# Attention in one launch: value products one half step at a time, maxima turned by VectorE, sums copied in halves

## The reference

```python
qkv = x @ W_attn + b_attn
q, k, v = jnp.split(qkv, 3, axis=2)
...
scores = jnp.einsum('bhqd,bhkd->bhqk', qh, kh) * scale
scores = jnp.where(causal, scores, -jnp.inf)
probs = jax.nn.softmax(scores, axis=-1)
out = jnp.einsum('bhqk,bhkd->bhqd', probs, vh)
out = out.transpose(0, 2, 1, 3).reshape(B, S, D)
return out @ W_proj + b_proj
```

## Time and profile before

| | |
|---|---|
| three runs | 2105.65, 2110.08, 2115.99 us; median 2110.08 |
| profiled execution | 2109.09 us, its span 2107.4 us |
| PE busy | 2033.5 us (96%) |
| DVE busy | 1854.7 us (88%) |
| ACT busy | 1486.4 us (71%) |
| POOL busy | 475.0 us (23%) |
| exponentials, L1021 | 2176, 596 ns mean |
| maxima, L1047 | 960, 1220 ns mean |
| value products, L1232 | 8696 instructions, 694.6 us |
| DMAs on the SP queue | 157.92 MB, 25.9% of the 16 DMA engines' time |

### The profile page before, as it was taken

One profiled execution on the slowest core, in us unless ns is written; L12 is line 12 of the kernel. 1 busy time (PEld: TensorE's weight loads), 2 busy tenths in 40 slices (PEclk: granted clock), 3 DMA queues, 4 the chain that ended last, 5 costly groups with the idle time before them and its releaser, 6 DMA issues. The chain is left out here.

```text
span 2107.4 us, 46575 instructions
## 1 busy us (share of the span) xinstructions
PE 2033.5 (96%) x18225; PEld 1126.7 (53%) x18225; DVE 1854.7 (88%) x3143; ACT 1486.4 (71%) x2787; POOL 475.0 (23%) x637
## 2 busy tenths in 40 slices
PE   6987999999999999999999999999999989999998
PEld 5875444444444444444444444444444458888887
DVE  7988799999999999999999999999999738998996
ACT  2331388888888888888888888888888665555554
POOL 0000011011111111111011111101111127776774
PEclk9997799999999999999999999999999999999999
DMA  6896021121212112122121212212122122323320
GB/s 194 319 324 221 14 71 47 53 58 38 76 46 67 48 48 65 36 77 51 54 58 38 66 47 70 48 53 58 38 76 67 47 74 80 98 86 91 84 77 31
DMA packets 163004, 168.31 MB, mean 80 GB/s; under 512 B 74704, under 2 KB 102880, under 8 KB 162784
## 3 DMA queue, kind: packets, MB, share of 16 engines
q1 hardware_dynamic: 155072, 157.92, 25.9%
q10 hardware_dynamic: 7712, 7.41, 1.2%
HBM read 95.77 MB, written 67.63 MB: 78 GB/s over the span
## 5 line engine op out<-in xcount | busy, mean ns | idle before, releaser
L1021 ACT ACTIVATE probs<-ps_s 128x512 f32<-128x512 f32 x2176 | 1178.7, 596 | 243.2 <-PE ps_s L1211 215.6
L1047 DVE TENSOR_REDUCE maxes<-ps_m 128x2 f32<-128x1024 f32 (+1 forms) x960 | 1142.7, 1220 | 104.9 <-PE ps_m L1174 82.5
L1232 PE MATMUL ps_acc<-probs,vs 128*32 128x256 f32 (+1 forms) x8696 | 694.6, 391 | 11.2 <-ACT acc_sb L999 11.2
L1211 PE MATMUL ps_s<-qs,ks 50*128 50x512 f32 (+3 forms) x2560 | 571.1, 444 | 0.8 <-ACT probs L1021 0.7
L1174 PE MATMUL ps_m<-ks,qs 48*128 48x512 f32 (+3 forms) x2560 | 498.7, 388 | 13.7 <-DVE maxes L1047 8.3
L1211 PEld LDWEIGHTS ps_s<-qs,ks 50*128 50x128 f32 x2560 | 251.4, 183 | 408.4 <-ACT probs L1021 373.4
L1232 PEld LDWEIGHTS ps_acc<-probs,vs 128*32 128x32 f32 x8696 | 172.8, 108 | 290.3 <-issue 188.9
L953 POOL TENSOR_SCALAR_AFFINE_SELECT probs<-probs 128x512 f32<-128x512 f32 x256 | 158.8, 635 | 721.9 <-ACT probs L1021 718.0
L1174 PEld LDWEIGHTS ps_m<-ks,qs 48*128 48x128 f32 x2560 | 260.9, 189 | 90.5 <-DVE maxes L1047 70.9
L1054 DVE CUSTOM_DVE_ANT_0 sums_masked<-ps_m,mask 128x384 f32<-128x384 f32 (+1 forms) x512 | 186.6, 420 | 21.7 <-PE ps_m L1174 5.7
L1425 POOL TENSOR_TENSOR hid<-square,hid 128x512 fp32r<-128x512 f32 x128 | 175.4, 1382 | 97.6 <-DVE square L1436 85.7
(11 more groups left out here) (133 smaller groups left out, 1851.0 us busy)
## 6 DMA issues: line engine op xcount, KB each, us to landing
qs<-q_scr SPq DMA_DIRECT2D x384, 64.0 KB, 2.7
ks<-k_scr SPq DMA_DIRECT2D x384, 64.0 KB, 2.8
q_scr<-probs SPq DMA_DIRECT2D x32, 512.0 KB, 3.9
k_scr<-probs SPq DMA_DIRECT2D x32, 512.0 KB, 5.3
o_scr<-acc_sb SPq DMA_DIRECT2D x64, 256.0 KB, 2.9
v_scr<-probs SPq DMA_DIRECT2D x16, 512.0 KB, 6.0
v_dense<-v_scr SPq DMA_DIRECT2D x16, 512.0 KB, 4.5
o_in<-o_scr SPq DMA_DIRECT2D x32, 256.0 KB
```

The source lines that it names most:

```text
L1021: act.activation(probs[:, s % RING, x], ps_s[:, k % BANKS], ACT.Exp).then_inc(ring_taken, 1)
L1047: last = dve.tensor_reduce(maxes[c % 2][:, :, pairs, tt, i], banks, AX.X, ALU.max)
L1211: last = pe.matmul(ps_s[:, k % BANKS, at:at + width], ks[u][rows, j // TT, p, j % TT * P:(j % TT + 1) * P], qs[u][rows, c, p, q0:q0 + widt ...
L1232: last = pe.matmul(ps_acc[h * VW:(h + 1) * VW, q0:q0 + width], vs[u][:, j, h], probs[:, s % RING, h % banks_of(s), at:at + width], start=( ...
```

## The change

- **Value products.** They are now a list of their own (`VALUES`): two entries for a step of four banks, one for a step of two heads, 68 in all. Each half step does one entry, the one VALUES_BEHIND = 6 half steps back. Halves are 256 and 256 columns, in a mixed step 256 and 128 + 128; a two-head step's 256 are done in one.
- **Rows of maxima.** VectorE turns `max_parts` (128 x 32) in 32 x 32 blocks into `max_rows` (128 x 32: for each 32 queries the 32 rows of maxima). TensorE's transpose and ScalarE's copy go, and the ring holds scores alone. `store_rows` has eight DMAs of 2 KB in place of four of 4 KB: for each of four blocks of 32 queries and each of two row groups, 16 partitions of 128 bytes go into 2 partitions of eight pieces each.
- **Sums of values.** `ps_acc` is copied in two halves of 256 columns: the first after the mixed step's products, the second after the two-head step's, which touch the second half only. The two-head step's products wait for the first copy, the next chunk's first product for the second.

```diff
+VALUES_BEHIND = 6
...
 def halves_of(s):
     blocks = STEPS[s][2]
     j, q0, col, width = blocks[0]
-    if len(blocks) > 1:
-        return [blocks[:1], blocks[1:]]
-    return [[(j, q0, col, width // 2)], [(j, q0 + width // 2, col + width // 2, width // 2)]]
+    return [[(j, q0, col, 2 * P)], [(j, q0 + 2 * P, col + 2 * P, width - 2 * P)] + blocks[1:]]
+VALUES = [(s, halves) for s in range(NS) for halves in ([(0,), (1,)] if banks_of(s) == 4 else [(0, 1)])]
...
+def order(s, last):
+    got = []
+    for half in range(banks_of(s) // 2):
+        x = sum(banks_of(i) // 2 for i in range(s)) + half
+        y = x - VALUES_BEHIND
+        got += [("bank", 2 * half), ("bank", 2 * half + 1), *items_at(x), ("values", (y < 0, *VALUES[y % len(VALUES)]))]
+    return [(what, y) for what, y in got if not (last and what in ("item", "found", "rows") and y[0])]
+def acc_piece(s, halves):
+    if 1 not in halves:
+        return None
+    return 1 if s + 1 in CHUNK_END else 0 if s + 2 in CHUNK_END else None
...
+    sp.wait_ge(lead.acc_copied, 2 * (NCH * n + c + 1))
...
-        max_rows = [t.sb(f"max_rows{i}", [MROWS * GH * TT, P], F32R) for i in range(2)]
+        max_rows = [t.sb(f"max_rows{i}", [P, MROWS * GH * TT], F32R) for i in range(2)]
...
+        rows_turned, rows_in = t.sem("rows_turned"), [t.sem(f"rows_in{i}") for i in range(2)]
...
+        TURN = 32
+        ROWS = 2 * P // TURN
...
-            def store_rows(u, c, copied):
-                sp.wait_ge(ring_taken, copied)
-                for r in range(2):
-                    for a in range(MROWS):
-                        dst = qs[u][ROW * r + TERMS + a:ROW * r + TERMS + a + 1, c].rearrange("o p (t q) -> o (p t) q", q=P)
-                        row = (r * MROWS + a) * PAIRS * TT
-                        sp.dma_start(dst.bitcast(F32), max_rows[c % 2][row:row + PAIRS * TT, :].bitcast(F32)).then_inc(rows_in[c % 2], 16)
+            def store_rows(n, u, c):
+                sp.wait_ge(rows_turned, NCH * n + c + 1)
+                for i in range(P // TURN):
+                    for r in range(2):
+                        dst = qs[u][ROW * r + TERMS:ROW * r + TERMS + MROWS, c].rearrange("a p (t i q) -> a (p t) i q", i=P // TURN, q=TURN)[:, :, i]
+                        row = TURN * i + r * MROWS * PAIRS * TT
+                        sp.dma_start(dst.bitcast(F32), max_rows[c % 2][row:row + MROWS * PAIRS * TT, :].bitcast(F32)).then_inc(rows_in[c % 2], 16)
...
-                    opened += 1
-                    store_rows(0, x[1], opened)
+                    store_rows(0, 0, x[1])
...
-                            store_rows(*unit_of(x, n, u)[1:], taken(n, k))
-                        k += what in ("bank", "rows")
+                            store_rows(*unit_of(x, n, u))
...
-            def copy_rows(n, c, filled, k):
-                act.wait_ge(ring_filled, filled)
-                if not early(n, c):
-                    act.wait_ge(rows_in[c % 2], 16 * 2 * MROWS * halves(n, c))
-                act.copy(max_rows[c % 2][:], ps_s[0:MROWS * GH * TT, k % BANKS, 0:P]).then_inc(ring_taken, 1)
-            def copy_acc(n, c):
-                act.wait_ge(pv_done, NS * n + CHUNK_END[c])
-                if not early(n, c):
-                    act.wait_ge(acc_stored[c % 2], 16 * halves(n, c))
+            def copy_acc(n, s, piece):
+                c = STEPS[s][0]
+                act.wait_ge(pv_done, NS * n + s + 1)
+                if piece == 0 and not early(n, c):
+                    act.wait_ge(lead.acc_stored[c % 2], 16 * halves(n, c))
                     act.wait_ge(lead.sums_in[c % 2], 16 * GH * halves(n, c))
-                act.copy(lead.acc_sb[c % 2][:], ps_acc[:]).then_inc(acc_copied, 1)
-            opened = 0
-            for what, x in OPENING:
-                if what == "rows":
-                    copy_rows(0, x[1], opened + 1, opened)
-                    opened += 1
+                part = slice(2 * P * piece, 2 * P * (piece + 1))
+                act.copy(lead.acc_sb[c % 2][:, part], ps_acc[:, part]).then_inc(acc_copied, 1)
...
-                            unit, _, c = unit_of(x, n, u)
-                            copy_rows(unit, c, taken(n, k), k)
-                            k += 1
-                    if at := ended(s, PV_BEHIND, n, first):
-                        copy_acc(*at)
+                        elif what == "values" and not (first and x[0]):
+                            if (piece := acc_piece(*x[1:])) is not None:
+                                copy_acc(n - 1 if x[0] else n, x[1], piece)
...
+                    for s, parts in VALUES[-VALUES_BEHIND:]:
+                        if (piece := acc_piece(s, parts)) is not None:
+                            copy_acc(n, s, piece)
...
+            def turn_rows(n, c):
+                dve.wait_ge(max_parted, 2 * (NCH * n + c + 1))
+                if not early(n, c):
+                    dve.wait_ge(rows_in[c % 2], 16 * ROWS * halves(n, c))
+                dve.transpose(max_rows[c % 2][:].bitcast(F32),
+                              max_parts[c % 2][:].bitcast(F32).rearrange("p r a x -> p (r a x)")).then_inc(rows_turned, 1)
...
+                            unit, _, c = unit_of(x, n, u)
+                            turn_rows(unit, c)
...
-            def turn_rows(n, c, k):
-                pe.wait_ge(max_parted, 2 * NCH * n + 2 * (c + 1))
-                pe.transpose(ps_s[0:MROWS * GH * TT, k % BANKS, 0:P],
-                             max_parts[c % 2][:].bitcast(F32).rearrange("p r a x -> p (r a x)"), keep["ident"][:]).then_inc(ring_filled, 1)
...
-                    pe.wait_ge(rows_in[c % 2], 16 * 2 * MROWS * (halves(n, c) + 1))
+                    pe.wait_ge(rows_in[c % 2], 16 * ROWS * (halves(n, c) + 1))
...
-                        pe.wait_ge(acc_copied, NCH * n + c)
-                pieces = blocks if halves == (0, 1) else halves_of(s)[halves[0]]
+                        pe.wait_ge(acc_copied, 2 * (NCH * n + c))
+                    if s + 1 in CHUNK_END:
+                        pe.wait_ge(acc_copied, 2 * (NCH * n + c) + 1)
+                pieces = blocks if parts == (0, 1) else halves_of(s)[parts[0]]
                 for j, q0, col, width in pieces:
                     for h in range(GH):
                         at = h // banks_of(s) * (CH // heads) + col
                         last = pe.matmul(ps_acc[h * VW:(h + 1) * VW, q0:q0 + width], vs[u][:, j, h],
                                          probs[:, s % RING, h % banks_of(s), at:at + width],
-                                         start=(j == 0 and 0 in halves), stop=(s + 1 in CHUNK_END), skip_group_check=True)
-                if 1 in halves:
+                                         start=(j == 0 and 0 in parts), stop=(s + 1 in CHUNK_END), skip_group_check=True)
...
-                        elif what == "rows":
-                            unit, _, c = unit_of(x, n, u)
-                            await_bank(n, k, first)
-                            turn_rows(unit, c, k)
-                            k += 1
-                        elif what == "values" and s >= PV_BEHIND:
-                            values(n, u, s - PV_BEHIND, x, last)
+                        elif what == "values" and not x[0]:
+                            values(n, u, *x[1:], last)
                         elif what == "values" and not first:
-                            values(n - 1, 1 - u, NS + s - PV_BEHIND, x, False)
+                            values(n - 1, 1 - u, *x[1:], False)
                         elif what == "values":
                             fill(pe, keep["w_o"], ps_acc[:], 2)
...
-                    for s in range(NS - PV_BEHIND, NS):
-                        values(n, u, s, (0, 1), True)
+                    for s, parts in VALUES[-VALUES_BEHIND:]:
+                        values(n, u, s, parts, True)
```

More of the change, by code:

```diff
@@ L1285, in _ @@
                         fill(pe, keep["w_o"], ps_acc[:], 3)
-                elif what == "rows":
-                    turn_rows(0, x[1], opened)
-                    opened += 1
             def body(n, u, first, last):
```

35 lines of the change are left out of this document (11 added, 24 removed).

## The result

The changed kernel takes 2301.2 us (median of 4 runs, 2283.71 to 2326.53), the kernel before beside it 2110.63 (4 runs, 2105.65 to 2115.99): ratio 1.0875, with an interval of 1.0794 to 1.0956. It is slower, as forecast, but by 190 us instead of 28, and far outside the range of 2085 to 2160. The profiled execution took 2308.57 us, its span is 2306.9.

A forecast was written before the change was run, and what follows sets the result against it. TensorE's order of work was taken as the bound, SyncE's queue directly under it. Per unit, 90.6 - 2.9 + 4.9 of waits = 92.6 us; fifteen units +30, the last -1.35, giving 2138 us, range 2085 to 2160.

The forecast's parts named there:

- c: SyncE's queue: time from one row DMA's issue to the next, taken as 0.65 us, bounds 0.47 and 0.77.
- both waits: TensorE waits 1.55 us for rows before chunk 3's scores, 3.35 for loads before the next unit's chunk 2 maxima: 4.9.
- The 1.8 to a row DMA's landing: SyncE's rows of maxima: the last row DMA lands 1.8 us after its issue starts, as the sums' copy does.
- TensorE's own gain: Attention unit: TensorE's terms sum to -2.9 us, so left to itself it would need 87.7 per unit instead of 90.6.
- the half copies: Accumulator copied in two halves: 0.1 us for each of eight waits, 0.8 per unit, ends 0 and 0.25 each.
- the whole copy: Accumulator copy at chunk ends: its old hold-up of some 1.15 us per unit goes; net -0.35 with the new copies' waits.
- the turn on VectorE: Rows of maxima turned on VectorE: 0.2 us each, bounds nothing and 0.6, costing TensorE nothing but starting row DMAs later.
- the pieces of 128 + 128: Value products of mixed half steps on TensorE: 0.63 us each; re-cutting the pieces takes 6.7 to 6.5, -0.2 per unit.
- the last unit: Last attention unit, which loads no successor: only the first wait, -2.9 + 1.55 = -1.35 us.
- The queue isn't felt: Rival on SyncE: loads get ahead or issue overlaps, only TensorE's gain of 46 us is left, 2064; chance 0.06.
- The issues are cheap: Rival on SyncE: row DMAs cost 0.47 us like loads, waits 2.0, unit 89.7, about 2094; chance 0.12.
- The gain fails as well: Rival: VectorE falls behind or copy waits cost 0.25 each, while the waits stay; 94.5 per unit, 2168; chance 0.13.

The follow-up runs named there:

- e4: The kernel before with each row DMA cut in two (eight of 2 KB per chunk), nothing else: 2287.63 us, ratio 1.0730 to the kernel before.
- e3: The changed kernel with chunk rows turned and sent two half steps earlier and the loads around them moved to either side: 2063.93 us, ratio 0.9769 to the kernel before.
- e6: The kernel before with VectorE's turn, eight row DMAs and e3's places, keeping the old product order and whole copies: 2077.95 us, ratio 0.9859.
- e7: The changed kernel's product order and half copies, with the kernel before's TensorE transposes, ScalarE copies and four row DMAs: 2085.7 us, ratio 0.9889.
- e1: The changed kernel with dummy products of 512 columns, 6 and 13, ahead of its two waits on DMAs: 2167.53 us, ratio 1.0262 to the kernel before.
- e10: e3 with TensorE made to wait once per unit for ScalarE to read the scores just made, no late DMA: 2137.0 us, ratio 1.0090 to the kernel before.
- e11: e3 with TensorE made to wait for ScalarE in three half steps running, once per unit: 2269.16 us, ratio 1.0724 to the kernel before.
- e9: e1 with VectorE's turn of chunk 3's rows put ahead of the ternary weights in the last unit: 2148.77 us, ratio 1.0187 to the kernel before.

## Why the prediction was wrong

**Right, on SyncE.** c = 0.65 held (0.65 to 0.67), and with it the reading of the earlier trace rows that a DMA which leaves SBUF costs the queue more than a load. The queue did set both waits: 1.46 where 1.55 stood, and where 3.35 stood 3.1 to 3.3 in six units (1.2 to 2.8 in three, 4.0 to 5.0 in three, 2.7 on average). The 1.8 to a row DMA's landing was taken from the sums' copy, as no row gives it; it fits here, as the eighth issue begins at about 933.2 and the scores at 935.0. The Trainium skill's sentence in "DMA: Bandwidth & Descriptors", section "Issuing engines are not separate DMA queues", that starting a DMA is "usually small relative to the DMA itself", does not hold here: e4 loses 154 us to four more issues per chunk. In three units (lengths 109.7, 105.4 and 93.5) the second wait was under 0.3, because a low clock behind the first had given the queue time.

**Right, on TensorE's own gain.** 87.7 per unit was predicted; e3 shows 87.8 to 88.4. Of its terms the half copies (0.8 for eight waits) measured 0.18 and 0.02 per chunk end, 0.8 in all, the whole copy 0.2 to 0.3 more (0.35 predicted); the turn on VectorE took 0.20, as assumed; the pieces of 128 + 128 cost what 256 do. For these the sum has 0.63, which no row shows and its own line doesn't give (twice 0.36 is 0.72); they measured 0.58. e6 and e7 have the two halves of the gain as 1.6 and 1.1 for 1.5 and 1.3, so the total came near because the two missed in opposite directions.

**Wrong, and the cause of the miss: a wait was priced at its own length.** The prediction says of the two waits that "ScalarE and VectorE run dry in them, so neither has anything to catch up", and adds 4.9 per unit. It looked for the waits' consequence on the engines' queues and not on TensorE's clock. The granted clock falls to 0.50 within 2 us of a wait's end or inside the wait and stays there for 3.4 to 95.6 us. The term that is missing, the clock's, stood at nothing in the sum and is 169 us in the units; e1, which keeps the waits and fills them, measures it as 134 us in the medians, and lands within 1.5% of the predicted 2138. With that term (134 to 169) 2138 would have been 2272 to 2307. Could the trace of before have shown it? Not in its attention units. They are, in one stretch, the granted clock behind the busy times:

```profile
250.00:1600.00 1350.00, 1337.86 (x13820) 585.60 (x13824) 1240.00 (x1955) 1128.25 (x2140) 184.46 (x368) 1.00 0.21 55
```

The clock is 1.00 throughout, and the longest idle time of TensorE in it is the 0.70 of the earlier trace rows. But ahead of the units and behind them the same trace has waits of the size in question. TensorE, idle time in brackets, and then the stretches behind them with the granted clock after the busy times:

```profile
141.40 0.99 PE L749 MATMUL ps_t<-ident,xn 128*128 128x128 f32 x5 [2.73 <-DVE xn L419]
1718.19 1.20 PE L354 MATMUL ps_m<-ident,mxn 128*128 128x128 f32 x7 [2.98 <-DVE mxn L480]
```

```profile
141.80:145.20 3.40, 3.40 (x13) 2.92 (x12) 3.40 (x8) 1.17 (x2) 0.00 (x0) 0.50 1.03 265
1718.80:1725.60 6.80, 4.53 (x14) 3.36 (x12) 2.75 (x6) 2.83 (x6) 1.01 (x2) 0.50 0.47 122
```

Within a microsecond of the end of both waits the clock fell to 0.50, for 3.4 and 6.8 us. It did so after one of 1.80 (to 165.44) and one of 1.75 (to 1738.23) as well, for 3.4 each, and not after one of 1.62 (to 154.12). So the trace of before did show that waits of this size can bring the clock down. What it could not show is how long a low lasts in the attention units.

The Trainium skill has the kind of thing, in "TensorE: Matmul & The Clock Gate", section "A second HAM failure mode: psum-queue depth-cycling": short idle times between groups of products make the clock swing and cost throughput. e10 and e11 agree with it. I did not weigh it, and by it a rival with the clock's loss would have had to stand beside the others.

**Wrong: the last unit.** "The last one has only the first wait: -2.9 + 1.55 = -1.35." The turn was moved to VectorE, and what VectorE does at that moment was read only for the middle units. In the last unit it stands behind the ternary weights: a wait of 15.31 instead of 1.55, and 18.6 us more from this unit's start to the end. e9 shows the place to be the cause: with the turn ahead of the weights the distance is 2.68, and from the last unit's start to the end are 497.1 us.

**The sum again.** Predicted span 2136, measured 2306.9, 171 more: clock +169, last unit +20, waits -12 (62 for 73.5), TensorE's own gain -1 (45 for 43.5), opening -3 (the first unit begins at 241.0 instead of 243.9), which leaves -2 for roundings.

**The rivals.** "The queue isn't felt" is what e3 builds, and its 2064 is what e3 took. "The issues are cheap" fell with 0.65. "The gain fails as well" gave 2168, near the result of e1 by chance only: the gain did not fail.

**Open.** What decides whether a wait of 1.2 to 1.5 us brings the clock down (9 of 15 in e10), and how long it then stays (3.4 to 99 us). The lows of neighbouring units with equal waits differ by a factor of five and more. They are not without order: of the fifteen in e11 five last 10.2 us, five 17.1 and three 34.1, and the two longest, 95.6 in the kernel after and 99.0 in e11, both end 50.1 us behind the first scores of the next unit. So the place in the unit seems to bear on where a low can end; no run here tests it.

## What to carry to other kernels

Where TensorE is full and at full clock, an idle time of one to three microseconds in a loop cost here three to four times its length, the wait included (62 us of waiting and 169 of the clock in the changed kernel, 205 for 60 of waiting in e11); give it a term for the clock, look in the trace of before for what the clock did after waits in any stage, and look at the granted clock ahead of the busy shares when a result is worse than its waits. When small DMAs are added to a queue, lay out the issues with their start-to-start times up to the one a full engine waits for, and move the ones with room out of the way: the change lost 9% with its issues in the old places and gained 2.3% with the same DMAs in new ones. When work moves to another engine, read that engine's queue in the first and the last turn of the loop too.

## What the runs showed of the hardware

- The granted clock of a TensorE that was busy at 9.76 of 10.00 us fell from 1.00 to 0.50 some 0.6 us after the end of an idle time of 3.08; after one of 1.17 it did so in 9 of 15 cases (e10), and in 15 of 15 where up to three of them came in three half steps (e11). It stayed down for 3.4 to 99 us; in the longest low of the kernel after, 95.6 us from 521.9, TensorE was busy all through.
- Products whose results nobody reads, 3.25 us of them in a gap of 4.2 us, kept the clock at 1.00 in all fifteen units of e1, with at most 0.98 of idle time left; in e9, with 2.04 left in one unit, it fell there.
- A DMA from SBUF to SBUF of 2 KB holds SyncE for 0.65 to 0.67 from issue to issue, one of 4 KB for 0.68: the number counts here, not the bytes.
- VectorE turns 128 x 32 numbers of float32 in 32 x 32 blocks in 0.20 us.
